# One fp32 tensor for O^T, split into its two parts in the output stage, and one bias product of 128 rows

## The reference

```python
Q, K, V = xn @ Wq + bq, xn @ Wk + bk, xn @ Wv + bv      # 16 heads, Q and K of 2*64 columns, V of 64
P = softmax(Q1 @ K1.T / 8) - lam * softmax(Q2 @ K2.T / 8)
Y = concat(P @ V) @ Wo + bo                             # 1024 -> 256 columns
attention = 0.2 * ((Y - mean(Y)) * rsqrt(var(Y) + 1e-5) * gamma + beta)
experts = prob_of_best * (gelu(xn @ w1[e] + b1[e]) @ w2[e] + b2[e])   # e = best of 8 experts, per row
```

## Time and profile before

| | us |
|---|---|
| median of 3 runs (lowest to highest) | 1902.37 (1900.29 to 1905.68) |
| the profiled execution | 1902.98 |
| its span, first to last instruction | 1901.1 |
| PE busy in the span | 1832.4 (96%) |
| DVE busy | 1534.1 (81%) |
| ACT busy | 1398.9 (74%) |
| POOL busy | 709.4 (37%) |
| moved by DMA | 446.11 MB, mean 235 GB/s |

### The profile page before, as it was taken

One profiled execution on the slowest core, in us unless ns is written; L12 is line 12 of the kernel. 1 busy time (PEld: TensorE's weight loads), 2 busy tenths in 40 slices (PEclk: granted clock), 3 DMA queues, 4 the chain that ended last, 5 costly groups with the idle time before them and its releaser, 6 DMA issues. The chain is left out here.

```text
span 1901.1 us, 33183 instructions
## 1 busy us (share of the span) xinstructions
PE 1832.4 (96%) x10688; PEld 1422.6 (75%) x10688; DVE 1534.1 (81%) x2562; ACT 1398.9 (74%) x3287; POOL 709.4 (37%) x789
## 2 busy tenths in 40 slices
PE   5899999999999999999999999999999799999997
PEld 4677777777777777777777777777767699999886
DVE  7798888888888888888888888889977476666365
ACT  6798888888888888888888888888877476666000
POOL 2344222233222223332332223332392475654343
PEclk9999999999999999999999999999999799999999
DMA  9998888888888888888888888888876476666997
GB/s 290 267 253 244 234 226 228 230 222 226 233 223 227 231 215 223 225 232 225 229 229 224 226 227 228 228 230 223 211 200 181 139 285 238 234 234 218 304 370 272
DMA packets 229236, 446.11 MB, mean 235 GB/s; under 512 B 27936, under 2 KB 120992, under 8 KB 223072
## 3 DMA queue, kind: packets, MB, share of 16 engines
q1 hardware_dynamic: 225344, 434.06, 81.2%
q0 software_dynamic: 3744, 10.23, 1.9%
HBM read 184.40 MB, written 58.46 MB: 128 GB/s over the span
## 5 line engine op out<-in xcount | busy, mean ns | idle before, releaser
L608 ACT ACTIVATE e<-p_score,nmax 128x512 f32<-128x512 f32 x1024 | 697.3, 689 | 137.6 <-DVE nmax L840 137.2
L459 POOL TENSOR_SCALAR e<-e,rrec,lam 128x512 f32<-128x512 f32 x512 | 393.7, 769 | 957.1 <-DVE rrec L800 957.1
L840 DVE TENSOR_REDUCE nmax<-p_score 128x2 f32<-128x1024 f32 x512 | 623.3, 1217 | 154.1 <-PE p_score L949 152.2
L949 PE MATMUL p_score<-ks,qs 128*128 128x512 f32 x2048 | 579.8, 405 | 10.6 <-DMA ks<-k_parts 7.9
L949 PEld LDWEIGHTS p_score<-ks,qs 128*128 128x128 f32 x2048 | 365.3, 188 | 181.1 <-issue 52.0
L807 DVE SCALAR_TENSOR_TENSOR pm<-e,rrec 128x512 f32<-128x512 f32 x512 | 394.6, 771 | 10.5 <-issue 9.9
L912 PE MATMUL p_proj<-xh,w 128*128 128x512 f32 x1024 | 385.4, 417 | 7.5 <-POOL xl L441 4.6
L541 ACT COPY pT<-p_tr 128x512 f32<-128x512 f32 x512 | 301.0, 588 | 115.7 <-PE p_tr L961 112.5
L961 PE MATMUL p_tr<-consts,pm 128*128 128x128 f32 x2048 | 309.7, 274 | 3.9 <-ACT pT L541 3.0
L961 PEld LDWEIGHTS p_tr<-consts,pm 128*128 128x128 f32 x2048 | 250.2, 140 | 81.9 <-issue 19.5
L976 PE MATMUL p_pv<-pT,v 128*64 128x512 f32 x1024 | 249.6, 609 | 0.7 <-ACT pT L541 0.7
(11 more groups left out here) (157 smaller groups left out, 1864.1 us busy)
## 6 DMA issues: line engine op xcount, KB each, us to landing
ks<-k_parts SPq DMA_DIRECT2D x512, 256.0 KB, 4.6
qs<-q_parts SPq DMA_DIRECT2D x512, 128.0 KB, 4.2
w<-weight_parts_scratch SPq DMA_DIRECT2D x56, 1024.0 KB, 10.5
w<-in_w SPq DMA_DIRECT2D x46, 1024.0 KB, 6.3
oT_scratch<-oT SPq DMA_DIRECT2D x64, 512.0 KB
op<-oT_scratch SPq DMA_DIRECT2D x32, 1024.0 KB
wv<-weight_parts_scratch SPq DMA_DIRECT2D x56, 256.0 KB, 5.6
weight_parts_scratch<-w SPq DMA_DIRECT2D x8, 1024.0 KB, 6.4
```

The costliest lines, as they stand in the source:

```text
L459: nc.gpsimd.tensor_scalar(e2, e2, rrec[:, g % 4, 1:2], lam[:, 0:1], ALU.mult, ALU.mult).then_inc(s_e2, 1)
L608: nc.scalar.activation(ex[:, g % EX, m, :], p_score[g % 2][:, m, :], ACT.Exp, bias=nmax[:, g % 2, m:m + 1], accum_out=rsum[:, g % 4, m:m + ...
L840: vec.tensor_reduce(nmax[:, g % 2, :], p_score[g % 2][:, :, :], AXX, ALU.max, negate=True).then_inc(s_max, 1)
L949: last_op = nc.tensor.matmul(p_score[g % 2][:, m, :], qs[j][u][:, m, qt * P:(qt + 1) * P], ks[j][u][:, m, part, :], start=(part == 0), sto ...
```

## The change

- `oT` becomes one fp32 tensor of 128 x 512, written by ACT alone; DVE's `low_o` leaves the attention stage, the waits for it become waits for ACT's copy, and the stored tensor is half as large.
- In the output stage a group's O^T is one DMA of 1 MB into one of two buffers `of`. ACT makes the high part of all 8 pairs of heads (`high_o`), DVE the low part of pairs 0 to 3 and POOL that of pairs 4 to 7, into one of two buffers `op` (three before). PE waits for both low parts. The places of these calls in the queues stand in the diff.
- The two bias products of one contraction row become one of 128 rows, with ones against a tile whose row 0 is the bias's high part, row 32 its low part, and all others zero. DVE writes the two rows into `bo_rows`, and ACT copies them into `bop`.
- SP stores results three groups late instead of two.

```diff
-                                [("oT", [P, 2, S], F32R)])
+                                [("oT", [P, S], F32)])
...
             def store_o(pair):
                 batch = batch_of(pair)
-                sp.wait_ge(s_olo, pair + 1)
-                sp.dma_start(oT_d[pair % PAIRS, :, :, batch * S:(batch + 1) * S], oT[:, :, :].bitcast(F32)
-                             ).then_inc(s_ost, 16)
+                sp.wait_ge(s_o, pair + 1)
+                sp.dma_start(oT_d[pair % PAIRS, :, batch * S:(batch + 1) * S], oT[:, :]).then_inc(s_ost, 16)
...
-                nc.scalar.copy(oT[:, 0, :], p_pv[:, :]).then_inc(s_ohi, 1)
+                nc.scalar.copy(oT[:, :], p_pv[:, :]).then_inc(s_o, 1)
...
-                if st == 2 and pair >= 2:
-                    low_o(pair - 2)
-                if g == STEPS - 1:
-                    low_o(NPAIRS - 2)
...
-            low_o(NPAIRS - 1)
...
-                        pe.wait_ge(s_olo, pair)
+                        pe.wait_ge(s_o, pair)
...
-        OPS = 3
+        OPS, LOW_ON_DVE, LATE = 2, PAIRS // 2, 3
...
             def load_o(n):
-                for c in range(2):
-                    sp.dma_start(op[n % OPS][:, c, :, :].bitcast(F32), oT_v[:, c, :, n * G:(n + 1) * G]
-                                 ).then_inc(s_op[n % OPS], 16)
+                if n >= OPS:
+                    sp.wait_ge(s_olo, n - OPS + 1)
+                    sp.wait_ge(s_olo_pool, n - OPS + 1)
+                sp.dma_start(of[n % OPS][:, :, :], oT_v[:, :, n * G:(n + 1) * G]).then_inc(s_op[n % OPS], 16)
...
             for n in range(GROUPS):
                 if n + OPS < GROUPS:
-                    sp.wait_ge(s_oy, n + 1)
                     load_o(n + OPS)
-                if n >= 2:
-                    store_out(n - 2)
-                    if n - 2 + R < GROUPS:
-                        load_x(n - 2 + R)
+                if n >= LATE:
+                    store_out(n - LATE)
+                    if n - LATE + R < GROUPS:
+                        load_x(n - LATE + R)
...
             nc.gpsimd.memset(ones[:, :], 1.0).then_inc(s_ones, 1)
+            nc.gpsimd.memset(bo_rows[:, :], 0.0).then_inc(s_ones, 1)
...
+            def low_o(n):
+                pool.wait_ge(s_ohi, n + 1)
+                a = LOW_ON_DVE
+                nc.gpsimd.tensor_tensor(op[n % OPS][:, 1, a:, :], of[n % OPS][:, a:, :],
+                                        op[n % OPS][:, 0, a:, :].bitcast(F32), ALU.subtract).then_inc(s_olo_pool, 1)
+
             pool.wait_ge(s_scaled, 1)
+            low_o(0)
+            low_o(1)
             for n in range(R):
                 add_beta(n)
...
                 fetch(n)
                 if n >= R:
                     add_beta(n)
+                if n + OPS < GROUPS:
+                    low_o(n + OPS)
...
-                nc.scalar.copy(bop[:, 0, :], rows[0:1, 0, :]).then_inc(s_wohi, 1)
+                nc.scalar.copy(bop[:, :], rows[:, 0, :]).then_inc(s_wohi, 1)
                 act.wait_ge(s_ones, 1)
                 nc.scalar.copy(ones_r[:, :], ones[:, :]).then_inc(s_wohi, 1)
+                act.wait_ge(s_bo, 2)
+                nc.scalar.copy(bop[:, :], bo_rows[:, :]).then_inc(s_wohi, 1)
+
+            def high_o(n):
+                act.wait_ge(s_op[n % OPS], 16 * (n // OPS + 1))
+                if n == 0:
+                    act.wait_ge(s_h, HG * (FFN_TILES - 1))
+                elif n == 1:
+                    act.wait_ge(s_w2lo, FFN_TILES)
+                else:
+                    act.wait_ge(s_oy, n - OPS + 1)
+                nc.scalar.copy(op[n % OPS][:, 0, :, :], of[n % OPS][:, :, :]).then_inc(s_ohi, 1)
...
             for q in range(GROUPS // 2):
+                for n in (2 * q + 2, 2 * q + 3):
+                    if n < GROUPS:
+                        high_o(n)
                 act.wait_ge(s_d, MOMENT_STEPS * q + RECIPROCAL_STEP)
...
                 dve.wait_ge(s_wohi, 2)
-                v.tensor_tensor(bop[:, 1, :], rows[0:1, 0, :], bop[:, 0, :].bitcast(F32), ALU.subtract
-                                ).then_inc(s_wolo, 1)
+                dve.wait_ge(s_ones, 2)
+                v.tensor_copy(bo_rows[0:1, :], bop[0:1, :].bitcast(F32)).then_inc(s_bo, 1)
+                v.tensor_tensor(bo_rows[BO_LOW:BO_LOW + 1, :], rows[BO_LOW:BO_LOW + 1, 0, :],
+                                bop[BO_LOW:BO_LOW + 1, :].bitcast(F32), ALU.subtract).then_inc(s_bo, 1)
...
             turns(body, after_third=output_weights)(dve)
+            low_o(0)
+            low_o(1)
...
                     if done[0] == RECIPROCAL_STEP:
+                        if 2 * q + 3 < GROUPS:
+                            low_o(2 * q + 3)
                         base(2 * q)
                         base(2 * q + 1)
...
                     last_op.then_inc(s_bn, 1)
+                    if n == 0:
+                        low_o(OPS)
...
                     normed(2 * q + c)
+                if 2 * q + 4 < GROUPS:
+                    low_o(2 * q + 4)
                 for c in range(2):
                     result(2 * q + c)
...
-                pe.wait_ge(s_op[c], 32 * (n // OPS + 1))
+                pe.wait_ge(s_olo, n + 1)
+                pe.wait_ge(s_olo_pool, n + 1)
...
-                    for part in range(2):
-                        nc.tensor.matmul(p_o[r][:, s, :], ones_r[:, :], bop[:, part, :],
-                                         start=(part == 0), stop=False)
+                    nc.tensor.matmul(p_o[r][:, s, :], ones_r[:, :], bop[:, :], start=True, stop=False)
```

More of the change, by code:

```diff
@@ L192, in front_stage @@
         s_rec, s_e2, s_comb = sem("a_rec"), sem("a_e2"), sem("a_comb")
-        s_tr, s_pT, s_pv, s_ohi, s_olo = sem("a_tr"), sem("a_pT"), sem("a_pv"), sem("a_ohi"), sem("a_olo")
+        s_tr, s_pT, s_pv, s_o = sem("a_tr"), sem("a_pT"), sem("a_pv"), sem("a_o")
         s_lam, s_bq = sem("a_lam"), sem("a_bq")
@@ L808, in combine @@
                                          in1=ex[:, g % EX, 1, :], op0=ALU.mult, op1=ALU.add).then_inc(s_comb, 1)
[L810 to L813, removed]
             statistics(0)
@@ L923, in values @@
                 if with_logits(n) and n >= 3:
-                    pe.wait_ge(s_olo, n - 2)
+                    pe.wait_ge(s_o, n - 2)
                 if it < QT:
@@ L1096, in ffn_and_output_stage @@
         sb("w1p_home", [P, 2, KT, F])
-        op1, op0, op2 = (sb(f"op{c}", o_shape, F32R) for c in (1, 0, 2))
+        op0 = sb("op0", o_shape, F32R)
+        of = [sb(f"of{c}", [P, PAIRS, G]) for c in range(OPS)]
+        op1 = sb("op1", o_shape, F32R)
         sb("loads_home", ahead.rest)
-        op = [op0, op1, op2]
+        op = [op0, op1]
         w2p = [sb(f"w2p_{j}", [P, 2, FT, E], F32R) for j in range(2)]
@@ L1105, in ffn_and_output_stage @@
         wo, wop = sb("wo", [P, PAIRS, E]), sb("wop", [P, 2, PAIRS, E], F32R)
-        rows, bop = sb("rows", [P, 3, E]), sb("bop", [1, 2, E], F32R)
-        ones, ones_r = sb("out_ones", [1, P]), sb("ones_r", [1, P], F32R)
+        rows, bo_rows, bop = sb("rows", [P, 3, E]), sb("bo_rows", [P, E]), sb("bop", [P, E], F32R)
+        ones, ones_r = sb("out_ones", [P, P]), sb("ones_r", [P, P], F32R)
+        BO_LOW = 32
         gamma, beta = rows[:, 1, :], rows[:, 2, :]
@@ L1127, in ffn_and_output_stage @@
         s_op = [sem(f"o_op{c}") for c in range(OPS)]
+        s_ohi, s_olo, s_olo_pool = sem("o_hi"), sem("o_lo"), sem("o_lo_pool")
         s_x, s_ff, s_ost = ([sem(f"o_{w}{r}") for r in range(R)] for w in ("x", "ff", "st"))
@@ L1205, in _ @@
             out_v = out.rearrange("(n s p) e -> n p s e", s=2, p=P)
-            oT_v = oT_d.rearrange("h p c t -> p c h t")
+            oT_v = oT_d.rearrange("h p t -> p h t")
             def load_x(n):
@@ L1227, in first_o @@
                 load_o(0)
-                sp.wait_ge(s_h, HG * (FFN_TILES - 1))
                 load_o(1)
             turns(body, before_last=first_o)(sp)
-            sp.wait_ge(s_w2lo, FFN_TILES)
-            load_o(2)
             store(FFN_TILES - 1, 0)
@@ L1241, in _ @@
                 if n + OPS < GROUPS:
-                    sp.wait_ge(s_oy, n + 1)
                     load_o(n + OPS)
-                if n >= 2:
-                    store_out(n - 2)
-                    if n - 2 + R < GROUPS:
-                        load_x(n - 2 + R)
-            store_out(GROUPS - 2)
-            store_out(GROUPS - 1)
+                if n >= LATE:
+                    store_out(n - LATE)
+                    if n - LATE + R < GROUPS:
+                        load_x(n - LATE + R)
+            for n in range(GROUPS - LATE, GROUPS):
+                store_out(n)
             for r in range(R):
@@ L1398, in output_weights, with low_o @@
                 dve.wait_ge(s_wohi, 2)
-                v.tensor_tensor(bop[:, 1, :], rows[0:1, 0, :], bop[:, 0, :].bitcast(F32), ALU.subtract
-                                ).then_inc(s_wolo, 1)
+                dve.wait_ge(s_ones, 2)
```

(19 more changed lines are left out.)

2 lines of the change are left out of this document (added).

## The result

The changed kernel takes **1911.54 us** (median of 5 runs, 1907.49 to 1914.35), the kernel before 1901.94 us beside it: ratio 1.0055, interval 1.0042 to 1.0068. It is slower by 0.55%, as forecast (1911). But its profiled execution is the fastest of its five, 1907.49 us, 4.5 us above that of before (1902.98). The traces can explain those 4.5 us, not the other 5 between the medians.

The account below looks back on a forecast made before the run. The output stage was taken to run at DMA's pace, PE close behind. Terms 8.0 + 1.5 - 0.7 = +8.8 us on the profiled 1902.98 gave 1911.8, and 1911 us as that execution is 0.6 above the median; range 1887 to 1919.

Parts of the forecast that it names:

- What bounds the kernel: Attention stage: PE full, removed DVE work hidden; output stage: DMA sets the pace, 15.5 us per two groups, PE close behind.
- The bias product, 0.125 us: Output stage: the new product takes 0.125 us (upper bound 0.215), so a group falls from 6.88 to 6.27 us.
- Exclusion at the port: Output stage: two-SBUF-input DVE instructions and POOL's readers take turns, 16.7 us per pair of groups; +8.0 us (-1.0 to +17.6), chance 0.58.
- The first four groups have their parts in time.: Start of the output stage: the first four groups run at PE's 6.27 us each, 25.1 us together.
- Clock, taken as 0 within the stage: Output stage: PE's slow clock behind waits makes a group up to 8.0 us, hidden under half of 16.7: 0 us.
- ScalarE's wait, +1.5 (0 to +3.5): Expert stage, tile 3: ScalarE waits for DVE's bias rows, delaying GELUs and pausing PE some 2.0 us, less 0.44: +1.5 us.
- End of attention, -0.7: End of the attention stage: DVE's last low part no longer stands ahead of the change of stage; bounds -0.7 and 0.
- Tail 0, up to +1.5: Behind the last group: same instructions, taken as 0; up to +1.5 us if DVE enters it late.
- PE as the bound: Output-stage rival: POOL's readers fall into DVE's waits and PSUM work, 6.27 us a group; 1886 to 1894 us, chance 0.27.
- Loads late: Output-stage rival: loads of 11.81 us make 17.3 us per pair; 1915 us, 1920 with slow clock; chance 0.05 (late or clock).
- The same pace: Output-stage rival: port work at its lower bound, 15.2 us a pair against 15.5 before; 1897 to 1908 us, chance 0.10.

Follow-up runs that it names:

- Experiment 5: Kernel before with only the bias product of 128 rows, ScalarE's last bias copy behind its expert tiles, O^T still in two parts: 1910.06 us, 1.0035.
- experiment 1: Changed kernel with the whole low part of O^T on DVE, none on POOL: 1896.86 us, 0.9966 of the kernel before.
- experiment 2: Changed kernel with the whole low part of O^T on POOL, none on DVE: 1927.11 us, 1.0127 of the kernel before.
- experiment 3: Changed kernel with POOL's low part left out from group 2 on (PE multiplies stale parts): 1889.55 us, 0.9923; output stage 104.8 us.
- experiment 4: Changed kernel with POOL's low part replaced from group 2 on by a memset into an unused buffer: 1900.24 us, 0.9988; output stage 112.0 us.
- experiment 7: Changed kernel with ScalarE's wait for DVE's bias rows and its last bias copy moved behind the expert tiles: 1915.14 us, 1.007.
- experiment 9: Changed kernel with bias rows and Wo's low part made between DVE's first two low parts, ACT's bias copy behind its second high part: 1912.69 us, 1.0068.
- experiment 11: Changed kernel with output weights prepared late and loads of groups 2 and 3 ahead of the expert stage's last store: 1910.24 us, 1.005.
- experiment 6: Changed kernel with loads of O^T from group 2 on issued from ScalarE's queue instead of SP: 1910.03 us, 1.0043.

## Why the prediction was right, point by point

- **What bounds the kernel.** Right. PE's full attention stage swallowed the removed DVE work; the output stage was at DMA's pace. Experiment 5 shows it best: 16 groups at 5.9 us instead of 6.88, no change in the stage.
- **The bias product, 0.125 us.** 0.12 measured, not the 0.215 by which few rows cost as much as 128. Missed was that the 24 products behind it get cheaper too, so a group is 5.9 us, not 6.27.
- **Exclusion at the port.** The mechanism is shown by experiments 1 to 4. A pair with low parts to come was put at 16.7 us; from 1797.8 to 1879.1 us five pairs took 16.3 each. What I mis-sized most is the count: I took six equal pairs, but a pair's time runs to the start of the next and holds any wait ahead of that, while the last pair ends with PE's last product: 14.0 us. First four groups 24.7 us (25.1), though only because a cheaper group (5.9 us) and an unforeseen wait (1.0) nearly cancel. 24.7 + 81.3 + 14.0 is 120.0 against my 125.3: +2.7 where I had +8.0, of which 2.7 for the last pair, 2.2 for the five others and 0.4 at the start. The five are 15.0 to 18.4 us each, and 16.7 was a choice between two bounds, so that their mean agrees owes something to luck. With the same shares for DVE and POOL, experiments 7, 9 and 11 gave 116.1, 121.9 and 124.4, so one profiled execution fixes this term no better than to some 4 us; and in all four kernels it was the fastest of five.
- **"The first four groups have their parts in time."** Not quite: group 2's load was issued at 1774.5, behind the last store of the expert stage on SP, and PE waited 1.00 us. I had counted the waits of these loads, but not their place in the queue.
- **Clock, taken as 0 within the stage.** Four halves of 4.3 to 4.6 us are seen, in four pairs out of eight; behind each PE waits for a low part again within two groups, so most of it seems hidden, as forecast; no run takes it away.
- **ScalarE's wait, +1.5 (0 to +3.5).** +1.9 for tile 3, pause 2.07 us as worked out. In experiments 1, 2, 3 and 6 the same pause was followed by slow products, and tile 3 took 15.6, +3.4: the upper bound. Not seen at all was that without it a worse collision waits (experiments 5 and 7).
- **End of attention, -0.7.** PE's pause at the change of stage fell from 2.60 to 1.44 us: -1.2, in this trace and in every run without DVE's low part in the attention stage (1.44 or 1.45 us), while experiment 5, which keeps it there, has 2.60. The term was right in kind and too small. The time to the start of tile 3 fell by 1.9 us; the rest I can assign to no row, and between the runs this time varies by more than that.
- **Tail 0, up to +1.5.** +1.7, a little above the bound: DVE enters it late, with the first moments of its last pair at 1895.7 instead of 1891.5.
- **The rivals.** PE as the bound would need the port free: experiment 3 comes to 104.8, not 100. Loads late: none of PE's ten waits names the load, and the last chain passes over a load once; experiment 6 speaks against it too, if not cleanly. The same pace: not met, at 16.3 us a pair, though three of the six pairs took 15.0 to 15.7.

So the sum, +4.5 between the profiled executions where I had +8.8, was high; the medians, at +9.6 us, agree with it partly by luck. The other 5 us are 4.0 by which the change's profiled execution lies below its median and 1.0 by which that of before lies above; they are in no trace.

## What to carry to other kernels

When work moves from one engine to another, look at which ports it reads, not only at which engine has time. Two SBUF inputs on VectorE and a reading GpSimd follow one another, so half of the work on the idle engine cost more than all of it on the busy one. And before a wait is taken out, ask what it keeps apart: here removing one brought a 5 us collision, and a stage that began sooner met a load held in another queue.

## What the runs showed that I had not expected

- A bias product of one contraction row slows its neighbours: 24 products behind it took 3.01 us, behind one of 128 rows 2.82 (experiment 5).
- A GpSimd write delays VectorE's TENSOR_SCALAR of 128x4 to 2.20 us, while a subtraction of two SBUF inputs passes at 1.21 us (experiment 4).
- A GpSimd gather took 8.10 us and ended with a run of back-to-back VectorE instructions, and that delay shielded PE's path. Another gather passed such a run in 2.65 us; what decides isn't shown.
- The same pause of PE, 2.07 us, was followed by 24 products in 3.10 us in one execution and in 4.31 in another:

```profile
1533.20 4.31 PE L1510 MATMUL p_h<-xsp,w1p 128*128 128x256 f32 x24 [2.07 <-ACT h L1311]
```

This is the kernel of experiment 1; the row of the changed kernel, at 1533.44, is in the section on the result.
